# A finer step in the written-out order of a four-layer graph-attention kernel: the head attention yields twice, and the order strings are new

## What is computed

```
h = relu(layernorm(x));  x = x + gnn_l(h)          # l = 0..3
# one attention: Wh = h @ W; s = Wh @ a1; t = Wh @ a2
# e[i, j] = leaky_relu(s[i] + t[j]), masked by adj; out = softmax_j(e) @ Wh
```

## Time and profile before

| | |
|---|---|
| median of three runs | 2929.61 us (2924.24 to 2930.2) |
| the profiled execution | 2929.61 us, span 2927.8 us |
| granted TensorE clock, mean | 0.993 |
| instructions | 66974 |
| TensorE busy | 2867.1 us, 98% |
| VectorE busy | 2450.5 us, 84% |
| ScalarE busy | 2306.8 us, 79% |

### The profile page before, as it was taken

One profiled execution on the slowest core, in us unless ns is written; L12 is line 12 of the kernel. 1 busy time (PEld: TensorE's weight loads), 2 busy tenths in 40 slices (PEclk: granted clock), 3 DMA queues, 4 the chain that ended last, 5 costly groups with the idle time before them and its releaser, 6 DMA issues.

```text
span 2927.8 us, 66974 instructions
## 1 busy us (share of the span) xinstructions
PE 2867.1 (98%) x25624; PEld 2639.1 (90%) x25624; DVE 2450.5 (84%) x7049; ACT 2306.8 (79%) x6303; POOL 208.9 (7%) x410
## 2 busy tenths in 40 slices
PE   8999999999999999999999999999999999999997
PEld 7899999999999999999999999999999998999986
DVE  6788888888888888888888888888888888888866
ACT  6678778777788787788787787777787877887776
POOL 2000000000000000000000000000000000000000
PEclk8999999999999999999999999999999999999999
DMA  2000000000000000000000000000000000000000
GB/s 80 1 9 16 16 16 16 16 1 16 16 16 16 9 9 16 16 16 16 2 16 16 16 16 16 2 16 16 16 16 9 9 16 16 16 16 2 2 1 30
DMA packets 16367, 42.06 MB, mean 14 GB/s; under 512 B 5296, under 2 KB 6832, under 8 KB 16048
## 3 DMA queue, kind: packets, MB, share of 16 engines
q1 hardware_dynamic: 16048, 37.77, 3.7%
HBM read 20.99 MB, written 16.78 MB: 13 GB/s over the span
## 4 chain that ended last, share of the span: by engine, by line
PE 85%; ACT 9%; DVE 5%; issue 1%; SPq 0%; POOL 0%; DMA 0%
PE bank L515 45%; PE bank L584 23%; PE bank L620 7%; PE bank L536 4%; PE bank L572 3%; ACT junk L1022 3%; ACT junk L1031 2%; PE bank L672 1%; DVE O L916 1%; ACT Z L1175 1%; PE bank L560 1%; PE bank L698 1%; ACT Z L1068 1%; DVE oTlo L920 1%; ACT hT1hi L1177 0%
## 5 line engine op out<-in xcount | busy, mean ns | idle before, releaser
L584 PE MATMUL bank<-hw,R 128*128 128x257 f32 x3072 | 708.2, 381 | 1.7 <-ACT hw L1083 1.0
L584 PEld LDWEIGHTS bank<-hw,R 128*128 128x128 f32 x3072 | 566.5, 191 | 75.7 <-issue 3.6
L793 DVE SCALAR_TENSOR_TENSOR R<-bank,E,mask_ne 128x512 f32<-128x512 f32 x640 | 449.5, 743 | 3.2 <-PE bank L572 0.8
L1248 POOL TENSOR_TENSOR rs<-ve,mhalf 128x4 f32<-128x4 f32 x128 | 140.7, 1099 | 2661.2 <-DVE ve L745 1655.8
L1045 ACT ACTIVATE Z<-x,nm,rs 128x256 f32<-128x256 f32 x512 | 276.5, 594 | 53.0 <-DVE x L1010 32.1
L515 PE MATMUL bank<-wfc_hi,oThi 128*128 128x256 f32 (+1 forms) x1024 | 303.0, 296 | 0.0
L515 PE MATMUL bank<-wfc_hi,oTlo 128*128 128x256 f32 (+1 forms) x1024 | 289.6, 283 | 0.0
L515 PE MATMUL bank<-wfc_lo,oThi 128*128 128x256 f32 (+1 forms) x1024 | 289.5, 283 | 0.0
L620 PE MATMUL bank<-hw,R 128*64 128x65 f32 x8192 | 269.1, 224 | 0.3 <-DVE R L793 0.3
L620 PEld LDWEIGHTS bank<-hw,R 128*64 128x64 f32 x8192 | 251.1, 138 | 20.1 <-issue 9.9
L1068 ACT COPY Z<-bank 128x258 f32<-128x258 f32 (+1 forms) x512 | 180.8, 371 | 39.7 <-PE bank L515 39.3
(11 more groups left out here) (262 smaller groups left out, 8355.4 us busy)
## 6 DMA issues: line engine op xcount, KB each, us to landing
x<-in_x_dram SPq DMA_DIRECT2D x32, 512.0 KB, 3.4
out_dram<-x SPq DMA_DIRECT2D x32, 512.0 KB, 2.6
R<-in_adj_dram SPq DMA_DIRECT2D x2, 512.0 KB, 6.1
Z<-in_L_gnn_mlp_w_dram SPq DMA_DIRECT2D x2, 512.0 KB, 5.4
O<-in_L_gnn_W_fc_dram SPq DMA_DIRECT2D x1, 1024.0 KB, 7.0
R<-in_L_gnn_W_dram SPq DMA_DIRECT2D x1, 256.0 KB, 3.7
R<-in_L_gnn_W_hand_dram SPq DMA_DIRECT2D x1, 256.0 KB, 6.7
rowt<-in_L_gnn_W_dram SPq DMA_DIRECT2D x1, 256.0 KB, 4.7
```

The source lines that it names most:

```text
L584: ins = e.matmul(bk[:, 0:257], P[:, j, i * 128:(i + 1) * 128], hw[:, j, 0:257], start=(j == 0), stop=(j == NBLK - 1))
L793: e.scalar_tensor_tensor(P[:, t, :], bank_of(b, "row", p)[:, :], m["E"][:, 1, h, j:j + 1], mask[:, j, :], ALU.max, ALU.mult).then_inc(up(" ...
L1248: e.tensor_tensor(m["rs"][:, :], m["ve"][:, :], mhalf[:, :], ALU.pow).then_inc(up("rs", b))
```

## The change

In layer 0's head attention the `yield` moves into the loop over slices: a step ends after slices 1 and 3, so that a head is two steps (a and b). TensorE's sequence has 104 steps for each batch instead of 100. All order strings are replaced, for all five engines. No instruction and no wait is added or taken away; `FIRST`, `ENDS` and everything else stay.

```diff
--- before.py
+++ after.py
@@ TURNS["pe"], the cycle
-        ("1120011101001010112200112212212021122220221111111121101122110021122121211112021121111122212122111111"),
+        ("2221100111010010101102201122122002112102222222111111111100112211002211211221111200021111111221221222"
+         "1111"),
@@ TURNS["dve"], the cycle
-        ("2222221122200222111221220110101122010000010202100022221111211121112122102221121101100110110211012211"
-         "11111111110100000222111220022001012002021211122122"),
+        ("1222222221122202022111212201101000110221000010020200122221121112211111212221112012010011011011112221"
+         "11111111111101002202001110022202010102011122122222"),
@@ TURNS["act"], the cycle
-        ("2022021001220022121122012202220011222120122122112212212221121112211222102211112222112112111110212211"
-         "122222211202112121012111211122100002"),
+        ("0200221121120112020221211022122002201122210212212211222212121202121121212121221111222211122111111220"
+         "112212122221120111011212122111211222"),
@@ -622,7 +623,8 @@
                                            start=(j == 0 and i == 0), stop=(j == NBLK - 1), skip_group_check=True,
                                            tile_position=(0, c))
                     ins.then_inc(up("att0", b))
-                yield
+                    if j % 2:
+                        yield
```

More of the change, by code:

```diff
@@ L69 @@
     "pe": (
[L70 to L79 removed]
+        ("wwww00ww000000w0000ww0w0w000w011w0ww1w11w1ww1000000ww00001w000w0001w11220010000000000001122001001000"
+         "0111200020000002001100000121111121001000101011011220000000111111111211221100212000011101211110220111"
+         "11110001001001111"),
@@ new lines @@
+        ("wwwwwww0000w00www00w00wwww0wwwwwwwww0110w11101w0w1w11w10000w00www1w0w000wwww020w00020000w02002002020"
+         "0000010000000000010020012021002000001100110011000000200010010011000100001001100001110100101011010100"
+         "100102011111010010110021111100010010100102110011112001110010110110"),
+        ("0200221121120112020221211022122002201122210212212211222212121202121121212121221111222211122111111220"
+         "112212122221120111011212122111211222"),
+        ("3533355454445543435554555455545343335554554354455554445455455444445555554455434454554544545444444355"
+         "5445455455354455344545454445445444333355334224242444344424324334442443324444334242424344334444333433"
+         "4334444343432433343334443333443334423443343444433424334332334343343342222432423133311133113232332323"
+         "3313321121333322333133232233323223232322332323222232312232323322232231323232323333322333122221232322"
+         "2232111132313210220002221220221021122022200122220221112202212211112221211212121211201121112110112221"
+         "2112210201122212210020000110000011022201201212110001011010100020110100100100100001000001000011211001"
+         "1100201000011120100201010000000010101001000011110000100001001011000101101000101011001100001001111110"
+         "0111000110100001001100101000"),
@@ L111 @@
     ),
     "pool": (
-        ("wwwwwwww0wwwwwwwww10w0w20"),
-        ("2202"),
-        ("5553444233132201010120"),
+        ("wwwww0wwwwwwwwww1ww0ww00"),
+        ("1222"),
+        ("45535444233132202101001"),
     ),
     "sp": (
-        ("0"),
-        ("32"),
-        ("2165544313200"),
+        ("001"),
+        ("21"),
+        ("10544322310"),
     ),
```

37 lines of the change are left out of this document (18 added, 19 removed).

## The result

The changed kernel takes 2957.69 us (median of 4 runs, 2956.36 to 2960.23) where the kernel before takes 2929.6 on the same chip: ratio 1.0101, 95% interval 1.0084 to 1.0118. It is 1% slower; the forecast was 2915.5 and faster.

A forecast was written before the change was run, and what follows sets the result against it. TensorE, busy 2867.1 of 2927.8 us, bounds the kernel. Regular part -10, end -3, start -1 and block borders +0.5 sum to -13.5, rounded -14, from 2929.61: 2915.5 us, range 2897 to 2934.

The forecast's parts named there:

- No work is added: Halving heads adds no matmuls, semaphores or bytes; four more TensorE blocks at 0.26 us a border, taken as 0.5 us.
- The filled wait: Half of head 2 moved behind top(4) brings sums(0) 0.65 us earlier a period, 0.74 at best, 0.3 at worst.
- T 1.00 earlier: T, when m2 ends and top(4) is due, comes 1.00 us earlier, 1089.80 instead of 1090.80.
- VectorE's part, L767: With two mask products and head 2's division no longer ahead, L767 is ready near 1088.9; top(4)'s 0.48 us lateness goes.
- ScalarE's part: If L1175 starts at T+0.3, row(7) is free at T+3.4; if no earlier than now, at T+4.07.
- second rival: Won and given back: L1175 starts no earlier (0.3 us a period) and m1 waits 0.3; 2928 us, chance 0.2.
- what is late next is L808: On VectorE a mask product and division now precede L808, putting sums(0) at T+4.05, where it was T+3.79.
- The new wait at `m1`: Only turn(0) lies between turn(1) and m1, so m1 waits 0.3 us a period, bounds 0 and 1.
- The rest of the cycle: Other moved steps, such as att0 head 0, row(2) and attend(1), change nothing, with 0.3 us a period either way.
- The end, -3: In the last 545 us the waits at attf and proj go; -3 us, from -7 to +3.
- slower, by `m1`: Rival: turn(1)'s copy and low part queue behind batch 10's steps, m1 waits 1.8 us a period; 2958 us, chance 0.13.
- The signs of being wrong: L1077 waited for longer than before, an L760 wait above 0.65 us a period, or the last 545 us growing.

The follow-up runs named there:

- Run 1: Old orders on every engine, each head halved with its two steps together, against the kernel before: 2927.19 against 2926.05 us, ratio 1.0001.
- run 3: Kernel before with only head 2's second half moved behind top(4) and VectorE's L767 group moved up among the mask products: 2940.57 us, ratio 1.0048.
- Run 8: Kernel before with the last of ScalarE's four sums and VectorE's variance step for that batch moved later: 2921.4 us, ratio 0.9985.
- 9: Run 8 with VectorE's maximum for top(4) and its split sums put forward: 2912.94 us, ratio 0.9953.
- 13: Changed kernel with VectorE's last mask product of head 3 (P3.3) ahead of the reductions that wait for top(4): 2971.24 us, ratio 1.0151.
- run 15: Run 12 with later sum and variance, earlier split sums, and P3.3 ahead of the reductions and writing the row tile: 2914.69 us, ratio 0.9953.
- run 16: Run 13 with P3.3 writing the row tile: 2957.78 us, ratio 1.0099.
- run 4: Changed kernel with layer 1's variance step on VectorE and normalising steps on ScalarE back at the end of the cycle: 2960.6 us, ratio 1.0119.
- run 5: Run 4 with TensorE's turn(1) also back ahead of attend(0)'s last block: 2944.87 us, ratio 1.0063.
- run 6: Changed kernel with one TensorE step moved, row(5) back behind a block: 2984.78 us, ratio 1.0199.
- 7: Changed kernel with the moves of run 5 and run 6, and VectorE's division of head 2 later: 2989.12 us, ratio 1.0214.
- 10: Run 5 with row(5), top(2) and the VectorE mask products beside them put back as before: 2981.95 us, ratio 1.0187.
- 11: Run 10 with ScalarE's fourth sum and VectorE's variance step later, and the split sums ahead of the second low part: 2973.94 us, ratio 1.0161.
- run 12: Three engines' orders: new from head 0 of att0 to sums(0), old from r3 to hs2; against the kernel before 2926.22 against 2928.45 us, ratio 0.9993.

## Why the prediction was wrong, by its steps

- **No work is added:** right. Run 1 prices the halving at nothing. The 0.26 for a block's border was not tried by itself. The Trainium skill (TensorEngine Tiling (Array Packing), Key Properties) has a change of mode drain TensorE. By the digits the halving alone adds no such change, so run 1's 1.0001 does not test this rule.
- **The filled wait, 0.65 at `sums(0)`:** failed in size; it was 0.30, the "0.3 at worst" of the prediction. In its terms, with T 5.46 us (24 products) behind the first step of `m2`, `row(7)` came at T+3.75 and not T+3.25, `sums(0)` at T+4.45 and not T+4.05. The points on L767, head 3 and L808 below say why.
- **T 1.00 earlier:** right, 0.95, but for a reason that I had not seen. I followed the inputs of `m2` and not those of `zT`, for which the half head was the cover (run 3: 0.60); that the new order has other work there was luck for my sum.
- **VectorE's part, L767:** failed. "so it is ready near 1088.9, ahead of 1089.80: the 0.48 goes" counted the instructions taken from in front of L767 and left out L745, which waits for ScalarE's sums. It is the "small step" of the paragraph "Who is late?", which took 1090.98 for VectorE's own work. 0.31 of 0.49 stayed; runs 8 and 9 show both causes. The Trainium skill (PSUM — Partial Sum Buffer, Engine vs sequencer instructions) calls VectorE's queue strictly first in, first out. The row of 1.52 us idle ahead of L747, with L769 0.08 behind, agrees, and shows what this costs a small step.
- **ScalarE's part:** right in kind. The evacuation starts 0.23 us before T, not 0.3 after it, and `row(7)` waits for nothing. But the second rival's "L1175 started just when its `m2` group was done" misread: the first group's last product started at 1089.88, and ScalarE was at its sums until 1090.88. Run 8 shows ScalarE waiting for TensorE in this place as soon as one sum is gone.
- **Head 3, left out:** it waits 0.61 in the two-bank lane, 0.20 a period, for the bank that P3.3 reads, behind the reductions. The sum has the one and a half heads run through.
- **"what is late next is L808":** right, with a cause that I missed. Not only the mask product and division stand ahead of it; P3.3 can't go earlier either, because the tile that it writes is read by the parted half head until then (runs 13 and 15). In run 15, with the tile free and the sums moved, the wait is 0.03; with the tile alone, in run 16, it is 0.47.
- **The new wait at `m1`:** right in kind, 0.66 and not 0.3. The bare chain is 0.40 (run 4), near the 0.3 that it was sized at; the rest is layer 1's normalisation, moved in front of the copy on ScalarE. I had looked for a queue on VectorE. The wait came with 0.12 at `turn(1)`.
- **The rest of the cycle, "nothing, with 0.3 a period either way":** the largest error. `row(5)` 0.42, `top(2)` 0.15, the projection 0.27, less 0.17 at `attf`: 0.67. "none had a wait before" says nothing of an order in which less work stands between a step and what it waits for: between `top(2)` and `row(5)` there were 1.7 us of work (eight products) and now 0.9 (four).
- **The end, -3:** it grew by 4. The waits of 1.7 and 2.3 us are gone, as forecast, but L573 waits 5.9 us there in all where L572 waited 2.5. **The start, -1:** it was 7 shorter in the profiled execution, but run 1 has a start as short in the old order; see the last section.
- **The sum:** 25 x (+1.3) instead of 25 x (-0.4). The rival "slower, by `m1`" gave 2958 and the kernel took 2957.7, but this is chance: its wait at `m1` was to be 1.8 us, and was 0.66; half of the loss lay elsewhere (run 5).
- **The signs of being wrong:** two of three came. L762 was waited for by 0.66 a period, just above 0.65, and the last 545 us grew; the third, a longer wait for L1077 (now L1079), did not: 6.2 us in the regular part against 6.5 before, at `row(5)` and no longer at `row(7)`.

Not settled: why the two-bank lane jams in runs 6, 7, 10 and 11. The waits name ScalarE's reading of the bank; run 12 shows that it doesn't when all three engines have the old order there. Which instruction in front of it is at fault was not tried.

## What to carry to other kernels

Work that covers a wait can be moved only if nothing else depends on it by memory: ask which tile or bank it keeps busy, who writes there next, and what is queued behind that writer. For each small step on which the bottleneck engine waits, list everything ahead of it in its own queue with what each of these waits for; the wait can set the time as well as the amount of work, and where both end together, as here, taking one away gains little. An order over several engines is one thing: putting back a part of it around `row(5)` cost 27 us on the new kernel (run 6) and 44 and 37 us on run 5 (runs 7 and 10), putting back the whole stretch on three engines gave 31.

## What the runs showed of the hardware

The start is not the same from run to run. With the same order of instructions it took 242.4 us in run 1 and 250.45 in the kernel before; the granted clock of this stretch was 0.99 there and 0.95 here. Windows of run 1:
```profile
0.00:242.40 242.40, 221.68 (x2094) 201.55 (x2094) 191.19 (x511) 175.49 (x469) 30.02 (x56) 0.99 0.10 32
```
Eight microseconds of a difference between two profiled executions can thus be the start alone, while the periods agree within 0.01 us (88.83 and 88.82). That made the period, not the total, the measure for runs of which one differs from the next by 5 us.
